# The b2 product over all 128 rows, with its own zeroed buffer, and the instruction order that goes with it

## What is computed

```python
C1, C2, C3 = (_route_combine_weights(xa, U, K_ROUTE, TAU) for U in (U1, U2, U3))
h = jax.nn.gelu(_mixture(xf, C1, W1), approximate=False)
y = _mixture(h, C2, W2) + C3 @ b2
```

## Time and profile before

| | us |
|---|---|
| time, median of 3 runs | 2767.86 (2764.50 to 2769.37) |
| profiled execution: its time | 2765.2 |
| profiled execution: span, first to last instruction | 2763.4 |
| PE busy | 2616.3 (95%) |
| DVE busy | 2207.7 (80%) |
| ACT busy | 1067.6 (39%) |
| POOL busy | 811.1 (29%) |
| granted TensorE clock, mean | 0.984 of full speed |

### The profile page before, as it was taken

The page is one execution under the profiler, slowest core; times in us unless marked ns, Lnnn a source line. Parts: engine busy times, 40 slices in busy tenths (PEclk is TensorE's granted clock), DMA queues, the critical chain, the costliest instruction groups (busy, mean ns, idle before and its releaser), DMA issues.

```text
span 2763.4 us, 59981 instructions
## 1 busy us (share of the span) xinstructions
PE 2616.3 (95%) x22949; PEld 2189.8 (79%) x22949; DVE 2207.7 (80%) x6135; ACT 1067.6 (39%) x1622; POOL 811.1 (29%) x829
## 2 busy tenths in 40 slices
PE   3899999999999999999999999999999999985999
PEld 3778788888888888888888888888888888863776
DVE  5677888888888888888888888888888888762554
ACT  3333434444444444433444444444444344322332
POOL 1000133322323232322332232323232232226444
PEclk9999999999999999999999999999999999986999
DMA  7644444444444444443444444444344333245997
GB/s 226 174 141 107 114 127 129 124 109 115 118 118 110 117 112 97 117 118 93 107 112 99 107 117 112 109 112 113 89 106 109 93 98 83 55 87 157 230 234 169
DMA packets 322210, 336.02 MB, mean 122 GB/s; under 512 B 46676, under 2 KB 302751, under 8 KB 321412
## 3 DMA queue, kind: packets, MB, share of 16 engines
q1 hardware_dynamic: 286404, 307.37, 42.8%
q0 software_dynamic: 33792, 18.52, 4.0%
q10 hardware_dynamic: 1728, 6.29, 0.7%
HBM read 191.65 MB, written 221.81 MB: 150 GB/s over the span
## 4 chain that ended last, share of the span: by engine, by line
PE 77%; DVE 12%; issue 4%; DMA 2%; ACT 2%; POOL 2%; SPq 1%; POOLq 0%; ACTq 0%; DVEq 0%
PE mixp L1386 35%; PE attn_out L1320 6%; PE second L1304 5%; DVE nm L978 4%; PE first L1286 4%; DVE hid L1070 3%; PE misc L1254 3%; PE misc L1212 3%; PE mixp L1488 3%; PE misc L1422 2%; PE misc L1331 2%; PE second L1507 2%; PE misc L1461 2%; PE misc L1350 2%; PE first L1443 2%
## 5 line engine op out<-in xcount | busy, mean ns | idle before, releaser
L793 ACT ACTIVATE exps<-second 128x1024 f32<-128x1024 f32 x512 | 525.4, 1026 | 770.9 <-PE second L1304 763.6
L678 POOL DMA_INDIRECT expert_slots<-row_mem,sidx x512 | 510.4, 997 | 820.1 <-PE first L1286 579.1
L1386 PE MATMUL mixp<-w_h,r_part_h 128*128 128x256 f32 x3072 | 664.2, 297 | 2.3 <-DVE r_part_l L888 1.1
L978 DVE TENSOR_REDUCE nm<-first 128x4 f32<-128x1024 f32 x504 | 614.3, 1219 | 24.8 <-PE first L1286 24.2
L1386 PE MATMUL mixp<-w_h,r_part_l 128*128 128x256 f32 x3072 | 609.8, 280 | 0.0
L1386 PE MATMUL mixp<-w_l,r_part_h 128*128 128x256 f32 x3072 | 609.3, 279 | 0.0
L1386 PEld LDWEIGHTS mixp<-w_h,r_part_h 128*128 128x128 f32 x3072 | 467.8, 189 | 43.4 <-issue 2.1
L1386 PEld LDWEIGHTS mixp<-w_l,r_part_h 128*128 128x128 f32 x3072 | 468.8, 188 | 0.0
L1386 PEld LDWEIGHTS mixp<-w_h,r_part_l 128*128 128x128 f32 x3072 | 468.6, 188 | 0.0
L1070 DVE SCALAR_TENSOR_TENSOR x_mem<-mixp,C,x_mem 128x256 f32<-128x256 f32 x768 | 332.6, 477 | 74.5 <-PE mixp L1386 67.5
L1070 DVE SCALAR_TENSOR_TENSOR hid<-mixp,C,hid 128x256 f32<-128x256 f32 x704 | 303.6, 477 | 54.4 <-PE mixp L1386 52.9
(11 more groups left out here) (236 smaller groups left out, 3593.1 us busy)
## 6 DMA issues: line engine op xcount, KB each, us to landing
kst<-k_parts SPq DMA_DIRECT2D x256, 192.0 KB, 4.1
qst<-q_parts SPq DMA_DIRECT2D x256, 192.0 KB, 4.5
q_parts<-nat_h SPq DMA_DIRECT2D x128, 256.0 KB
k_parts<-ctx_part_h SPq DMA_DIRECT2D x64, 256.0 KB, 2.5
k_parts<-nat_h SPq DMA_DIRECT2D x64, 256.0 KB, 5.6
q_parts<-nat_l SPq DMA_DIRECT2D x64, 256.0 KB
exps<-in_wgu SPq DMA_DIRECT2D x30, 384.0 KB, 4.2
expert_slots<-row_mem SPq DMA_DIRECT2D x16, 642.0 KB, 6.5
```

The source lines that it names most:

```text
L678: pool.e.indirect_dma_start(out=slots_dram, out_offset=bass.IndirectOffsetOnAxis(ap=sidx[b % 2][:, t, k:k + 1], axis=0), in_=row[b % 2][:, ...
L793: act.e.activation(exps[:, j % NU, :, :, :].rearrange("p k t s -> p (k t s)"), second[:, :, :].rearrange("p k s -> p (k s)"), ACT.Exp, sca ...
L978: dve.e.tensor_reduce(nm[u % 2][:, :, 2 * j:2 * j + 2].rearrange("p t k -> p k t"), (mixp_mem if in_mixp(b, kind, j) else first)[:, :, :]. ...
L1386: m = pe.e.matmul(mixp[q % 2][:, t * D:(t + 1) * D], src[i][:, dt, t * P:(t + 1) * P], wmix[n][j][:, l, dt, :], start=(k == 0), stop=(k == ...
```

## The change

The bias product takes the whole of `c3_mem`, a new buffer of 128 x 256 that POOL zeroes at the start and of which ACT's copy (L813) writes rows 64 to 99 in each batch, and the whole of `b_rows`. So both products of `u` have 128 rows of contraction, of which 92 contribute zero (rows 0 and 1 of `b_rows` meet zeros). To make room, the buffer `pw` goes: the two inputs that it held at the start now lie in `out_sb`, and ACT's first write of `out_sb` waits for the second step of `v_b`.

```diff
-        pw_mem = sb("pw", (P, D))
-        pw = pw_mem[0:64, :]
         B2 = slice(64, 64 + 3 * L)
-        b2_raw, b2 = pw_mem[B2, :], b_rows[B2, :]
+        b2 = b_rows[B2, :]
...
-        b_raw = out_sb[0:2, 0, :]
+        b_raw, pw, b2_raw = out_sb[0:2, 0, :], out_sb[0:64, 1, :], out_sb[B2, 1, :]
...
-        c3T = mT_mem[B2, :]
+        c3_mem = sb("c3T", (P, S), F32R)
+        c3T = c3_mem[B2, :]
...
             pool.e.memset(b_rows[:, :].bitcast(F32), 0.0).then_inc(*own.up())
+            pool.e.memset(c3_mem[:, :].bitcast(F32), 0.0).then_inc(*own.up())
...
-                    act.wait_ge(v_b, 1)
+                    act.wait_ge(v_b, 2)
...
-                        m = pe.e.matmul(misc[:, t * D:(t + 1) * D], c3T[:, t * P:(t + 1) * P], b2, start=True, stop=True)
+                        m = pe.e.matmul(misc[:, t * D:(t + 1) * D], c3_mem[:, t * P:(t + 1) * P], b_rows[:, :], start=True, stop=True)
```

More of the change, by code:

```diff
@@ new lines @@
+        "OOTOTOTwcCTOOTDOTdOTOOTOTTOTOTOTBOTOTTnOOTOTOTwcCTOOTDOTdOTOOTOTTOTOTOTBOTOTTnOOTOTOTwcCTOOTDOTdOTOOTOTTOTOTOT"
+        "BOTOTTnOOTOTOTwcCTOOTDOTdOTOOTOTTOTOTOTBOTOTTnOOTOTOTwcCTOOTDOTdOTOOTOTTOTOTOTBOTOTTnOOTOTOTwcCTOOTDOTdOTOOTOT"
+        "TOTOTOTBOTOTTnOOTOTOTwcCTOOTDOTdOTOOTOTTOTOTOTBOTOTTnOOTOTOTwcCTOOTDOTdOTOOTOTTOTOTOTBOTOTTnOOTOTOTwcCTOOTDOTd"
+        "OTOOTOTTOTOTOTBOTOTTnOOTOTOTwcCTOOTDOTdOTOOTOTTOTOTOTBOTOTTnOOTOTOTwcCTOOTDOTdOTOOTOTTOTOTOTBOTOTTnOOTOTOTwcCT"
+        "OOTDOTdOTOOTOTTOTOTOTBOTOTTnOOTOTOTwcCTOOTDOTdOTOOTOTTOTOTOTBOTOTTnOOTOTOTwcCTOOTDOTdOTOOTOTTOTOTOTBOTOTTnOOTO"
@@ new lines @@
+        "QtPfQQsRRvFPQGQhKQRRiQlQQPQRRQpQQPRRrckQtyQQQFPfQGQsRRvQQhKPRRiQlQQQRRPQQpQQPRRrckQtQyQQFPfQGQsRRvQQhKRRPiQQlQ"
+        "QPRRQQpQQPRRrckQtQyQQFPfQGQsRRvQQhKRRPiQQlQQPRRQQpQQPRRrckQtQyQQFPfQGQsRRvQQhKRRPiQQlQQPRRQQpQQPRRrckQtQyQQFPf"
+        "QGQsRRvQQhKRRPiQQlQQPRRQQpQQPRRrckQtQyQQFPfQGQsRRvQQhKRRPiQQlQQPRRQQpQQPRRrckQtQyQQFPfQGQsRRvQQhKRRPiQQlQQPRRQ"
+        "QpQQPRRrckQtQyQQFPfQGQsRRvQQhKRRPiQQlQQPRRQQpQQPRRrckQtQyQQFPfQGQsRRvQQhKRRPiQQlQQPRRQQpQQPRRrckQtQyQQFPfQGQsR"
+        "RvQQhKRRPiQQlQQPRRQQpQQPRRrckQtQyQQFPfQGQsRRvQQhKRRPiQQlQQPRRQQpQQPRRrckQtQyQQFPfQGQsRRvQQhKRRPiQQlQQPRRQQpQQP"
@@ new lines @@
+        "RRrckQtQyQQFPfQGQsRRvQQhKRRPiQQlQQPRRQQpQQPRRrckQtQyQQFPfQGQsRRvQQhKRRPiQQlQQPRRQQpQQPRRrckQtQyQQFPfQGQsRRvQQh"
+        "KRRPiQQlQQPRRQQpQQPRRrckQtQyQQFPfQGQsRRvQQhKRRPiQQlQQPRRQQpQQPRRrckQtQyQQFPfQGQsRRvQQhKRRPiQQlQQPRRQQpQQPRRrck"
+        "QtQyQQFPfQGQsRRvQQhKRRPiQQlQQPRRQQpQQPRRrckQtQyQQFPfQGQsRRvQQhKRRPiQQlQQPRRQQpQQPRRrckQtQyQQFPfQGQsRRvQQhKRRPi"
+        "QQlQQPRRQQpQQPRRrckQtQyQQFPfQGQsRRvQQhKRRPiQQlQQPRRQQpQQPRRrckQtQyQQFPfQGQsRRvQQhKRRPiQQlQQPRRQQpQQPRRrckQtQyQ"
+        "QFPfQGQsRRvQQhKRRPiQQlQQPRRQQpQQPRRrckQtQyQQFPfQGQsRRvQQhKRRPiQQlQQPRRQQpQQPRRrckQtQyQQFPfQGQsRRvQQhKRRPiQQlQQ"
@@ new lines @@
+        "LOoOSMOpOqPwrMMOxSMOyMMDMMOEuMOPMdMfOGMMOJevOSMOhMPHMMiSOMMOlMOmOPnMIMLMOoOSMMOpOqPrMwMOxSMOMyMMDMOEuMOPMdMfOG"
+        "MMOeJvOSMhOMPHMMiOSMMOlMOmOPnSMMIMOLoOMMOpOqPrMwMOSxMOMyMDMMEOuMOPMdMfOGMMOeJvOSMhOMPMHMiOSMMOlMOmOPnSMIMMOLoO"
+        "MMOpOqPrMwMOSxMOMyMDMMEOuMOPMdMfOGMMOeJvOSMhOMPMHMiOSMMOlMOmOPnSMIMMOLoOMMOpOqPrMwMOSxMOMyMDMMEOuMOPMdMfOGMMOe"
+        "JvOSMhOMPMHMiOSMMOlMOmOPnSMIMMOLoOMMOpOqPrMwMOSxMOMyMDMMEOuMOPMdMfOGMMOeJvOSMhOMPMHMiOSMMOlMOmOPnSMIMMOLoOMMOp"
+        "OqPrMwMOSxMOMyMDMMEOuMOPMdMfOGMMOeJvOSMhOMPMHMiOSMMOlMOmOPnSMIMMOLoOMMOpOqPrMwMOSxMOMyMDMMEOuMOPMdMfOGMMOeJvOS"
@@ new lines @@
+        "MhOMPMHMiOSMMOlMOmOPnSMIMMOLoOMMOpOqPrMwMOSxMOMyMDMMEOuMOPMdMfOGMMOeJvOSMhOMPMHMiOSMMOlMOmOPnSMIMMOLoOMMOpOqPr"
+        "MwMOSxMOMyMDMMEOuMOPMdMfOGMMOeJvOSMhOMPMHMiOSMMOlMOmOPnSMIMMOLoOMMOpOqPrMwMOSxMOMyMDMMEOuMOPMdMfOGMMOeJvOSMhOM"
+        "PMHMiOSMMOlMOmOPnSMIMMOLoOMMOpOqPrMwMOSxMOMyMDMMEOuMOPMdMfOGMMOeJvOSMhOMPMHMiOSMMOlMOmOPnSMIMMOLoOMMOpOqPrMwMO"
+        "SxMOMyMDMMEOuMOPMdMfOGMMOeJvOSMhOMPMHMiOSMMOlMOmOPnSMIMMOLoOMMOpOqPrMwMOSxMOMyMDMMEOuMOPMdMfOGMMOeJvOSMhOMPMHM"
+        "iOSMMOlMOmOPnSMIMMOLoOMMOpOqPrMwMOSxMOMyMDMMEOuMOPMdMfOGMMOeJvOSMhOMPMHMiOSMMOlMOmOPnSMIMMOLoOMMOpOqPrMwMOSxMO"
@@ new lines @@
+        "MyMDMMEOuMOPMdMfOGMMOeJvOSMhOMPMHMiOSMMOlMOmOPnSMIMMOLoOMMOpOqPrMwMOSxMOMyMDMMEOuMOPMdMfOGMMOeJvOSMhOMPMHMiOSM"
+        "MOlMOmOPnSMIMMOLoOMMOpOqPrMwMOSxMOMyMDMMEOuMOPMdMfOGMMOeJvOSMhOMPMHMiOSMMOlMOmOPnSMIMMOLoOMMOpOqPrMwMOSxMOMyMD"
+        "MMEOuMOPMdMfOGMMOeJvOSMhOMPMHMiOSMMOlMOmOPnSMIMMOLoOMMOpOqPrMwMOSxMOMyMDMMEOuMOPMdMfOGMMOeJvOSMhOMPMHMiOSMMOlM"
+        "OmOPnSMIMMOLoOMMOpOqPrMwMOSxMOMyMDMMEOuMOPMdMfOGMMOeJvOSMhOMPMHMiOSMMOlMOmOPnSMIMMOLoOMMOpOqPrMwMOSxMOMyMDMMEO"
+        "uMOPMdMfOGMMOeJvOSMhOMPMHMiOSMMOlMOmOPnSMIMMOLoOMMOpOqPrMwMOSxMOMyMDMMEOuMOPMdMfOGMMOeJvOSMhOMPMHMiOSMMOlMOmOP"
@@ L140 @@
+        "RMOQMSOQMlQOQOmRRPMSMIMQLMQMpQRqQMRyMMSMMMMtMFMMOGOMMJuOvOMKMMMPMOMIMOMLMOQMOMMQRPQyQRQQSQRQRSOOOOPOOOOQFQPQRQ"
         "GJQRQKQIQRRSSLFGJIKL"
```

119 lines of the change are left out of this document (44 added, 75 removed).

## The result

| | us |
|---|---|
| median of 4 runs after | 2843.02 (2841.50 to 2845.70) |
| median of 4 runs before, on the same chip | 2766.18 (2763.79 to 2769.37) |
| ratio | 1.0278, 95% interval 1.0260 to 1.0296 |
| profiled execution: its time, span | 2843.0, 2841.2 |

The changed kernel is 77 us slower. The forecast was 2757 and the range ended at 2781, so both the side and the range were wrong.

The account below looks back on a forecast made before the run. PE was taken as the bound, busy 73.74 of 74.64 us per batch, DVE close behind. Terms summed to -0.40 per batch, times 28 -11 us: 2754 profiled, 2757 for the median; range 2738 to 2781.

Parts of the forecast that it names:

- The bias product, -0.10: On PE, u costs 0.33 ahead of s2 and s1 and 0.23 between two experts: saves 0.10 us per batch.
- `d_up` and `h_turn`, -0.50: One s2 group moved ahead of d_up covers PE's idle there and some before v: -0.50 us per batch.
- The wait at `S`, +0.20: With an s2 gone behind v, S on PE waits for DVE to empty its bank: +0.20 us per batch.
- The fourth `max_rows`, -0.20: PE's wait at one max_rows for DVE's nmp goes, as DVE has one expert less before it: -0.20 per batch.
- The other new waits, +0.10 for all: Small waits of the other moved pieces, such as turns and the first P: +0.10 us per batch together.
- N for the next but one unit now stands ahead of the fourth P: On SP, N takes about 2 us while P's maxima reach SP only 0.7 after it: cost 0.
- SP and the queues ... I take +0.10: Late POOL copy delays load_ctx, query stores and maxima; chain ends 29.4 after v, s2 due 29.7: +0.10 per batch.
- The rival: SP's block decides: stores behind load_ctx's load fetch stored queries late, PE idles 1.1 per batch, 2779 us; chance 0.17.
- 0.3 us of margin in a chain of ten terms: In SP's chain from the late copy to the s2 that reads the maxima, only 0.3 us was to spare.
- Bounds of +1.1: Bounds on the SP and queues term: 0 to +1.1 us per batch around the +0.10 taken.

Follow-up runs that it names:

- e13: e1 with the bias product on PE moved from ahead of s2 and s1 to between them and an expert: 2774.39 us, ratio 1.0027.
- e2: Kernel before with all order strings of the changed kernel, bias product still on half rows: 2846.58 us, ratio 1.0288.
- e3: Changed kernel with the second N (loads of keys and queries) back behind the fourth P's maxima on SP: 2806.34 us, ratio 1.0147.
- e4: Changed kernel with POOL's copy of the values and SP's load_v back in their old places: 2815.75 us, ratio 1.0182.
- e7: Kernel before with only POOL's copy of the values moved late, behind the scatters: 2773.07 us, ratio 1.0019.
- e1: Changed kernel with all order strings of the kernel before, so the whole-row bias product alone: 2767.75 us, ratio 1.0003.
- e5: Changed kernel with both queue moves back (those of e3 and e4): 2781.59 us, ratio 1.0048.
- e6: Kernel before with one move on SP, the N behind the fourth P put ahead of it: 2794.40 us, ratio 1.0109.
- e10: Changed kernel with the whole SP and POOL strings of the kernel before: 2770.86 us, ratio 1.0016.
- e12: e5 with POOL's addition of the attention output moved later, behind two scatters again: 2761.26 us, ratio 0.9976.
- e8: e5 with DVE's scaling into xhat moved ahead of an out_turn and a reduction: 2822.17 us, ratio 1.0198.

## Why the prediction was wrong, step by step

- **The bias product, -0.10: not there.** In the changed kernel `u` costs 1252.82 - 1252.58 = 0.24, as forecast, but it cost no more before. The 0.33 came from comparing scores with an expert behind them with scores that have the router's product behind them. Behind the second of the scores of the earlier trace rows the next whole product starts 0.43 later even when no `u` stands ahead (e13, 1228.94 - 1228.51), against 0.33 in the earlier trace rows; why these two differ is not known. Without `u` these scores take 0.32 + 0.34 + 0.43 = 1.09, so `u` cost 1.32 - 1.09 = 0.23. Moving it with half rows would have cost 0.39 more (e2); the whole rows avoid that cost and save nothing against before.
- **`d_up` and `h_turn`, -0.50: right in cause, -0.34.** The wait at `d_up` (0.45 in every batch) is gone but once in 18. From `s2` to `v` 3.65 passed before and 3.66 pass after, with one more `s2` in between, so it is the gelu's chain on ACT that binds, as said. What is gained is the slot of that `s2` behind `v`, and that was 0.34 where the prediction had 0.43 to 0.50.
- **The wait at `S`, +0.20: right, +0.16.** It is too short for the list of named waits, but `S` starts 0.49 after `s1` where the step is 0.33, and 2.03 after `v`, just behind the 1.97 at which its bank is emptied.

```profile
1192.94 0.50 PE L1304 MATMUL second<-qst,kst 50*128 50x256 f32 x4
...
1196.60 0.63 PE L1212 MATMUL misc<-identr,hid 128*128 128x128 f32 x4
...
1198.14 0.50 PE L1286 MATMUL first<-kst,qst 48*128 48x256 f32 x4
1198.63 0.66 PE L1331 MATMUL misc<-identr,out_sb 128*128 128x128 f32 x4
```

- **The fourth `max_rows`, -0.20: right, -0.18.** The wait for `nmp` in the list is at another `P`, see the next item.
- **The other new waits, +0.10 for all: under-sized.** The second `P` waits 0.23 more, an expert's turn `m` 0.12 more. Against that `r_z` starts 0.16 sooner, which the prediction did not count.
- **"N for the next but one unit now stands ahead of the fourth P", costed at 0: this step failed most.** Its times of issue were right. It looked at when SP issues the maxima, not at what stands in front of them behind the issue: it cost 1.1 per batch on PE, 36.7 us (e3).
- **"SP and the queues ... I take +0.10": the term was mis-sized.** The copy and `load_ctx` came when forecast (20.0 against 20.1 after `v`). From the first store to the fetch of the stored queries 5.3 passed where I took 4.3 from the one row of before, and the fetch took 1.5 and not 0.8. 29.4 became 31.05, and 0.92 of idle time, 27.3 us (e4). The rival had this place, with a chance of 0.17. It took 1.1 of idle time, and 0.92 came; what it lacked was the other two losses. Its mechanism, stores close behind `load_ctx`'s load, fits the runs: where they are issued 0.42 behind it (the changed kernel, e2, e3, e7) the fetch follows the first store by 5.4 in the median, where they are 1.4 behind it (before, e1, e4, e5, e6, e10, e12) by 4.1 to 4.3.
- **DVE beside POOL: a term that wasn't there.** I counted what DVE does and in which order, and not which POOL instruction runs beside each. It cost 0.73 per batch on PE, 20.3 us (e12 against e5).

The three sum to 36.7 + 27.3 + 20.3 = 84, or 82 with both queue moves taken together; against 77 measured, the rest of the change is worth -5 to -7, and e12, which has none of the three, is 5.6 faster than before. Forecast for the same parts was -0.50 per batch, -14 us. The items above come to -0.34 + 0.16 - 0.18 + 0.35 - 0.16 = -0.17, -5 us. The difference is the bias product, the size of the `s2` slot and the small waits at `P` and `m`.

The lesson for the range: 0.3 us of margin in a chain of ten terms, each from one row, was written down and then treated as safe. Bounds of +1.1 stood beside it, but the forecast's chance was set as if only one such chain existed.

## What to carry to other kernels

Here a small DMA's landing depended on what was issued just ahead of it (3.0 us with 768 KB ahead, 1.7 without): when a bulk transfer passes a small one in the issuing string, charge the small one with it. In an order written out by hand each string fits only its partners, so for every moved DVE instruction look up what POOL does beside it, and read maxima of durations, not medians. A late copy that is nearly free where slack follows (5.4 us, e7) costs more where another move has used that slack (27.3 us, e4). When a piece's cost is read as a difference of two places, the pieces behind it must be alike too: here an unlike one made 0.10 of saving out of nothing.

## What the runs showed of the hardware

- A DVE `TENSOR_SCALAR` of 128 x 256 from SBUF to SBUF takes 0.407 us alone and up to 1.389 beside a POOL `TENSOR_TENSOR` of 128 x 512. Beside POOL's subtraction of 1.28 in e8 the pair takes 1.71, as beside the addition. The Trainium skill, "SBUF — State Buffer", section "Who interferes with whom", says that DVE in some of its modes and GpSimd share a pair of ports which the one that comes first holds for its whole instruction. The runs agree: in e8 POOL's instruction starts 0.05 first and `xhat` ends 0.15 after it. The one that had begun first hardly lost: POOL's addition has a median of 1.385 us with the collision, and 1.305 before and 1.304 in e12.
- A DVE CAST of 128 x 16 (`nmp`) has a mean of 169 ns before, 260 in the changed kernel, 262 in e8 and e12 and 194 in e10: the same instruction, beside other work of POOL and SP.
- Four DMAs of 4 KB behind four of 192 KB: 3.0 us from the end of the issues to the reader, against 1.7 without.
- The pair of bias products costs 0.23 with 36 rows beside other products of one half, 0.24 with 128 rows there, and 0.24 with 128 rows between two of 128. With 36 rows between two of 128 it costs 0.39 more: each step between whole and half rows adds about 0.1 (e2).

Not settled: whether it is the load of `load_ctx` that makes the stored queries take 5.4 and not 4.2 us to be fetched. The distance goes with how close behind that load the stores are issued in eleven kernels, and not with PE's order (e7), but in the four slow ones POOL's copy is late as well, and no run moves the load alone.
